# Six middle batches of an attention phase, written out as straight code instead of a loop over pairs of batches

## What is computed

```python
Q, K, V = layernorm(x) @ wq, ctx @ wk, ctx @ wv          # Q: 16 heads, K and V: 2 heads of 32
scores = rope(Q) @ rope(K).T / sqrt(32), masked
x = x + (softmax(scores) @ V) @ wo
n = layernorm(x)
top_v, top_i = top_k(n @ Wr + expert_bias, 2)
routed = sum over the two of softmax(top_v) * (silu(n @ Wg[e]) * (n @ Wu[e])) @ Wd[e]
x = x + routed + (silu(n @ Sg) * (n @ Su)) @ Sd
```

## Time and profile before

| | us |
|---|---|
| median of three runs | 1496.52 |
| the profiled execution, its own time | 1492.17 |
| its span, first to last instruction | 1490.1 |
| TensorE busy in the span | 1415.1 (95%) |
| VectorE, ScalarE, GpSimd busy | 984.5, 873.6, 548.2 |
| mean granted TensorE clock, share of full speed | 0.984 |

### The profile page before, as it was taken

One profiled execution on the slowest core, in us unless ns is written; L12 is line 12 of the kernel. 1 busy time (PEld: TensorE's weight loads), 2 busy tenths in 40 slices (PEclk: granted clock), 3 DMA queues, 4 the chain that ended last, 5 costly groups with the idle time before them and its releaser, 6 DMA issues.

```text
span 1490.1 us, 31015 instructions
## 1 busy us (share of the span) xinstructions
PE 1415.1 (95%) x8362; PEld 1104.3 (74%) x8362; DVE 984.5 (66%) x2692; ACT 873.6 (59%) x1994; POOL 548.2 (37%) x670
## 2 busy tenths in 40 slices
PE   6698999999999999999987899999999999999997
PEld 4575777776877767777665678878887888888885
DVE  4688888887889788897876666666663343334332
ACT  2589889887888878888895222222222443444342
POOL 2343331422323223233432242222233555455553
PEclk9899999999999999999998899999999999999999
DMA  5344454453454535444545222222236787886552
GB/s 166 106 109 130 120 151 146 133 155 113 139 161 113 164 115 147 146 118 134 177 140 174 95 86 85 86 85 86 86 128 185 186 190 185 258 193 110 108 85 36
DMA packets 141487, 198.49 MB, mean 133 GB/s; under 512 B 34943, under 2 KB 72575, under 8 KB 141314
## 3 DMA queue, kind: packets, MB, share of 16 engines
q1 hardware_dynamic: 119954, 158.33, 34.6%
q0 software_dynamic: 17952, 33.64, 11.9%
q10 hardware_dynamic: 3408, 4.46, 0.9%
HBM read 97.10 MB, written 69.35 MB: 112 GB/s over the span
## 4 chain that ended last, share of the span: by engine, by line
PE 85%; ACT 4%; issue 3%; DVE 2%; DMA 2%; SPq 2%; POOL 1%; ACTq 0%; DVEq 0%; POOLq 0%
PE psum L641 15%; PE psum L1407 13%; PE psum L1409 12%; PE psum L1408 12%; PE psum L750 7%; PE psum L731 7%; PE psum L686 4%; PE psum L687 4%; PE psum L688 4%; ACT a_probs L544 2%; PE psum L1474 2%; PE psum L656 2%; PE psum L1503 1%; PE psum L1403 1%; SPq L352 1%
## 5 line engine op out<-in xcount | busy, mean ns | idle before, releaser
L544 ACT ACTIVATE a_probs<-a_probs,a_low 128x512 f32<-128x512 f32 x512 | 370.2, 725 | 74.2 <-DVE a_low L895 73.1
L895 DVE CUSTOM_DVE_ANT_0 a_probs<-psum,a_bias 128x512 f32<-128x512 f32 x512 | 346.6, 685 | 92.2 <-PE psum L731 85.9
L641 PE MATMUL psum<-a_ident,a_probs 128*128 128x128 f32 x2048 | 313.1, 276 | 19.7 <-ACT a_probsT L550 6.4
L641 PEld LDWEIGHTS psum<-a_ident,a_probs 128*128 128x128 f32 x2048 | 244.6, 141 | 88.2 <-ACT a_probs L544 29.4
L731 PE MATMUL psum<-a_kT,a_q_stack 128*128 128x512 f32 x512 | 248.8, 487 | 9.0 <-issue 5.7
L550 ACT ACTIVATE a_probsT<-psum 128x512 f32<-128x512 f32 x344 | 203.7, 592 | 28.6 <-PE psum L641 28.6
L1276 POOL DMA_INDIRECT out<-b_y,b_pairs_sb x71 | 113.2, 1595 | 148.9 <-DMA out<-b_y,b_pairs_sb 88.9
L1712 DVE SCALAR_TENSOR_TENSOR b_v_hidden<-b_v_hidden,psum 128x256 f32<-128x256 f32 x71 | 29.9, 421 | 165.6 <-ACT b_v_hidden L1372 165.6
L471 POOL CAST a_w_hi<-a_w_raw 128x256 fp32r<-128x256 f32 x96 | 38.3, 399 | 264.7 <-DMA w_halves<-a_w_lo 260.4
L901 DVE COPY a_probsT<-psum 128x512 f32<-128x512 f32 x168 | 115.3, 686 | 19.2 <-PE psum L641 19.0
L750 PE MATMUL psum<-a_probsT,a_v 128*32 128x512 f32 x1024 | 118.9, 605 | 0.2
(11 more groups left out here) (206 smaller groups left out, 3164.2 us busy)
## 6 DMA issues: line engine op xcount, KB each, us to landing
b_w<-w_halves SPq DMA_DIRECT2D x16, 1536.0 KB
a_q_stack<-a_qT_hi SPq DMA_DIRECT2D x256, 64.0 KB, 2.0
a_q_stack<-a_qT_lo SPq DMA_DIRECT2D x256, 64.0 KB, 2.0
w_halves<-a_w_hi SPq DMA_DIRECT2D x96, 128.0 KB, 2.0
w_halves<-a_w_lo SPq DMA_DIRECT2D x96, 128.0 KB, 1.8
a_x_in<-in_x SPq DMA_DIRECT2D x32, 256.0 KB, 2.8
a_ctx_in<-in_ctx SPq DMA_DIRECT2D x32, 256.0 KB, 3.0
a_x_res<-in_x SPq DMA_DIRECT2D x32, 256.0 KB, 2.8
```

Of the source, the lines that this page charges most:

```text
L544: nc.scalar.activation(probs[:, h % 2, t], probs[:, h % 2, t], ACT.Exp, bias=low[:, h % H, t:t + 1], scale=-1.0, accum_out=total[:, h // G ...
L641: last = nc.tensor.transpose(out[:, P * i:P * (i + 1)], src(i), identity[:])
L895: nc.vector.tensor_tensor_reduce(probs[:, h % 2, t], psum[:, t % 2], bias[:, t], 1.0, HUGE, ALU.add, ALU.min, low[:, h % H, t:t + 1]).then ...
```

## The change

Both hardware loops become Python loops. Each engine's code then holds the "middle" stage six times, one after the other, and `b` is a number in each. The stages, their order, every compute instruction and every DMA stay as they are, and so do the totals that are waited for; the register instructions that work them out and the branches back to the loop's head are no longer there.

```diff
     def bodies(eng, body):
         body("start", -1, 1)
         body("first", 0, 0)
-        with eng.Fori(0, (B - 2) // 2) as i:
+        for i in range((B - 2) // 2):
             body("middle", 2 * i + 1, 1)
             body("middle", 2 * i + 2, 0)
         body("last", B - 1, 1)
```

```diff
         body("start", -1, 1)
         body("first", 0, 0)
-        with sp.Fori(0, (B - 4) // 2) as i:
+        for i in range((B - 4) // 2):
             body("middle", 2 * i + 1, 1)
             body("middle", 2 * i + 2, 0)
         body("middle", B - 3, 1)
```

## The result

The changed kernel takes 1487.97 us (median of five runs, 1487.27 to 1489.88); the kernel before, in the same comparison, 1496.52 us (1494.67 to 1498.89). The ratio is 0.994 with a 95% interval of 0.9927 to 0.9954: 8.55 us or 0.6% faster. Forecast were 1487.1 us and a range of 1483.5 to 1490.7.

A forecast was written before the change was run, and what follows sets the result against it. The prediction took TensorE's own work as the bound inside a batch; -8.9 us for the branches and -0.5 us for register sums gave -9.4 us, from the median 1496.52 to 1487.1 us, range 1483.5 to 1490.7.

The forecast's parts named there:

- The two branches, -8.93 us: TensorE's two taken branches in the middle batches go, with idle array and slow clock behind them: -8.93 us.
- the ruler: Distance between successive "out" starts, the period of one middle batch; the excess over six times 94.01 us was 8.93 us.
- The other engines' branches, nothing: Other engines' branches at the loop's end lie hidden under TensorE's gap: nothing; without that cover at most 2.90 us a time.
- Register sums, -0.5 us: Register sums before waits in the six middle batches go: -0.5 us, between nothing and 2.2 us.
- The slowing by EVENT_SEMAPHORE: Rival: TensorE's 103 waits a middle batch turn from 32 to 51 ns, time 1499.3 us; 2 in 100.
- Code traffic, nothing: The longer straight code fetches as much as the loops' 2.06 MB or a little less: nothing.
- "Last" and what follows move forward as one piece: Stages "last", "end" and the experts are unchanged and only move forward; a clock dip may shift 1.7 us either way.
- the 4.35 us: The profiled execution of the kernel before, 1492.17 us, stands 4.35 us under the median of its runs.
- The mislabelled releaser: Rival: at 332 us TensorE waits for ScalarE's exponentials, not the branch; gain at most 0.5 us, 1496.0; 3 in 100.
- The low clock did not come back elsewhere: Rival: slow stretches return at other waits; gain 6.3 us, time 1490.2 us; 9 in 100.
- The rival of somebody else's lag: At the loop's end pauses let GpSimd and SyncE catch up; half the gain goes, 4.5 us, 1492.0; 6 in 100.
- One sign that was set too wide: Between 145 and 720 us no gap on TensorE exceeds 0.5 us.

The follow-up runs named there:

- The kernel before, again: The kernel before, unchanged, run for a second profile: median 1495.98 us over 12 runs.
- the loops that run once: Against the changed kernel, each pair of middle batches sits in a hardware loop that runs once: 1490.70 us, in a second comparison 1486.63 us.
- late loads: The kernel before with SyncE's nine loads for the experts' phase at unit 12 of the last batch instead of unit 4: 1496.83 us, ratio 0.9989.
- one branch back: Against the kernel before, the four engines' loop makes two passes and batches 5 and 6 are written out: 1492.00 us, ratio 0.9959.

## Why the prediction was right

- **The two branches, -8.93 us.** Right, and it is nearly the whole result. The six batches gained 9.24 us between the two first profiles, and 8.56 us between the two second ones (572.42 less 563.86). How it splits was less certain than the text made it: the gap of 2.90 us was 2.88 to 3.51 us in other profiles, and the low clock, priced as an upper estimate of 1.7 us behind each, was missing in some. Using the ruler and not the sum of the parts kept the number whole, though the ruler too was laid on one execution; another, with longer gaps and one stretch of low clock instead of two, gave 0.6 us less.
- **The other engines' branches, nothing.** Right as a term, because all of them go at once. That TensorE's cover mattered is now measured: with TensorE straight and the others looping, each edge costs 2.4 us, within the 2.90 us named as the bound.
- **Register sums, -0.5 us.** Near in size, wrong in the owner. Where no edge disturbs them, batches 1, 5 and 6 took 282.02 us before and 281.92 after, in the second pair 282.14 and 281.99: 0.2 to 0.3 us in six batches. From "out" 0 to "out" 1 it went from 27.07 to 26.99 us, as the earlier trace rows foretold, but the text spoke of TensorE's ALU_OPs. It came from the other engines' sums: TensorE alone in registers gave 27.01 us, the others alone 27.08. The slowing by EVENT_SEMAPHORE that a rival feared is not there, and of the 103 waits a batch that it counted only 56 turned into one. The line of the transposes in the changed kernel, against the earlier trace rows:

```profile
L622 PEldq EVENT_SEMAPHORE  x333: 51/51/51, 58.8 to 794.2; - x167
```

- **Code traffic, nothing.** Right: 1.84 MB against 2.06.
- **"Last" and what follows move forward as one piece.** This is the step that failed in the profiled pair: from the last batch's first out to the end it was to be 771.2 us within a dip or two, and it was 778.1 us. The kernel before, again, took 779.6 us. The error was to take one profiled execution as the norm when it lay below every timed run; the text noted the 4.35 us and drew nothing from it. The median forecast did not suffer, since it was made from the median.
- **The rivals.** The mislabelled releaser, ScalarE's exponential, is refuted by the changed kernel and by the loops that run once: the same place, the same exponential, no gap; with TensorE alone in a loop the gap is back. The page Advanced Engine Details and Errata of the Trainium skill (section Control Flow Timing, about 108 ns) is nearer for a near target, where TensorE took 208 to 231 ns, than for a far one, where it took 3342 to 3962. The page Runtime: NRT & Kernel Launch (section Instruction fetch mechanics) has the rule that the trace bears out: only the jump out of reach stalls. GpSimd's jump over 253 instructions did not. The low clock did not come back elsewhere in the six batches, where it stayed at 1.00. The rival of somebody else's lag did not come true in the six batches; no period there exceeded 94.02 us.
- **One sign that was set too wide.** No gap over 0.5 us was to stand before 720 us. The wait of 2.00 us in the earlier trace rows is in the changed kernel too, 9 us behind the last batch's first "out" as before, and now falls at 718.9 us. Up to 710 us the largest gap was 0.41 us.

## What to carry to other kernels

Lay a ruler on a steady loop: the distance between two equal marks, pass by pass, gives the price of its back edge without any theory, while the parts (idle array, low clock, other engines' holes) overlap and vary. A branch back over a long body can stall an engine though its own record says 50 ns: look for the loop's first instruction behind it. With TensorE straight and the others looping more than half of the cost stayed. Count the body engine by engine: GpSimd, with the fewest instructions in the same loop, did not stall. And see in the instruction counts whether an experiment left in what it was to leave in; the loops that run once did not. Before reading a difference between two single profiles outside the part that changed, see where each profiled execution lies among its timed runs.

## What the runs showed of the hardware

- A taken branch to a far target takes TensorE's sequencer 3342 to 3962 ns, to a near one 208 to 231 ns; one that falls through, 67 to 83 ns. VectorE's and ScalarE's records show 34 to 63 ns in every case, and a far jump shows only as a hole until the loop's first instruction, of 3.1 to 3.6 us on VectorE, 3.2 to 3.9 on ScalarE and 2.5 to 2.8 on SyncE. GpSimd, with 253 instructions in a pass, has 217 to 250 ns.
- After a gap of 2.9 to 3.5 us on TensorE the granted clock was at its 1.2 GHz level for 3.4 us in some cases (both edges of the first profile of before, the first of two in its second profile and with late loads, the one edge with one branch back) and stayed at 2.4 GHz in others (the second edges of those two, both edges with the other engines straight). Gaps of 2.90 us were followed by it and one of 3.26 was not; nothing read here tells which.
- Register sums in front of nearly every wait of five engines cost 0.2 to 0.3 us in six batches of 94 us, as long as TensorE is the bound. TensorE's own, 867 ALU_OPs, cost nothing.
- The same kernel before had medians of 1496.5, 1497.6, 1498.2 and 1492.9 us in four comparisons, 5.3 us apart; differences of that size between kernels that were not timed together say nothing.
